# A selective scan on VectorE: two halves of the channels in one product, one scan and one multiplication by C

## The reference, cut to what matters

```python
# u_c, z: [token, 256]; dt_r, Bm, Cm come from u_c @ W_x.T (8, 16 and 16 columns)
dt = jax.nn.softplus(jnp.einsum('blr,dr->bld', dt_r, W_dt) + b_dt)
A = -jnp.exp(A_log)                                   # [256 channels, 16 states]
def step(h, inp):                                     # over the 256 tokens of a sequence
    dt_t, u_t, B_t, C_t = inp
    dA = jnp.exp(dt_t[..., None] * A)
    h = dA * h + (dt_t * u_t)[..., None] * B_t[:, None, :]
    y_t = jnp.einsum('bds,bs->bd', h, C_t)
    return (h, y_t)
y = (ys + u_c * D) * jax.nn.silu(z)
out = jnp.einsum('bld,ed->ble', y, W_out)
```

## Time and profile before

| | |
|---|---|
| Time, median of 3 runs | 628.76 us (628.01 to 629.89) |
| The profiled execution: its own time / its span | 627.47 us / 626.1 us |
| Scan phase, first drive to last scan | 279.1 to 526.7 us |
| Busy from 279 to 527 us (248 us): PE / DVE / ACT / POOL | 212.4 / 244.4 / 150.5 / 195.9 us |
| Busy from 527 to 626 us (99 us): PE / DVE / ACT / POOL | 83.0 / 36.9 / 30.9 / 26.7 us |
| Granted TensorE clock, as a share of full speed | 0.912 over the span, 0.96 in the scan phase |

### The profile page before, as it was taken

How to read it: one execution, slowest core, us unless ns; L and a number is a source line. 1 busy time by engine, 2 the same in 40 slices (tenths; PEclk the granted TensorE clock), 3 DMA queues, 4 the chain that set the end, 5 groups by cost and what they waited for, 6 DMA issues and landing times.

```text
span 626.1 us, 7242 instructions
## 1 busy us (share of the span) xinstructions
PE 516.1 (82%) x2146; PEld 285.0 (46%) x2146; DVE 445.5 (71%) x858; ACT 302.9 (48%) x562; POOL 314.0 (50%) x276
## 2 busy tenths in 40 slices
PE   1985777888877989889898998888787887679897
PEld 0732444556646855543233433323332432448655
DVE  5289978687232435549999999999999998424343
ACT  2654345345142532486774865755557541325421
POOL 0048433342441027026789778877899766310072
PEclk9996788788658999989999999989989898699999
DMA  8999900000003332021222121222221220023312
GB/s 299 413 332 331 311 30 1 1 1 19 21 28 106 112 90 54 6 70 58 79 71 69 67 66 67 72 63 71 83 67 68 84 69 4 17 69 93 115 51 85
DMA packets 31879, 58.09 MB, mean 93 GB/s; under 512 B 4384, under 2 KB 20256, under 8 KB 30944
## 3 DMA queue, kind: packets, MB, share of 16 engines
q1 hardware_dynamic: 29504, 52.06, 25.5%
q0 software_dynamic: 2048, 4.20, 2.4%
q10 hardware_dynamic: 288, 1.37, 0.7%
HBM read 50.27 MB, written 26.15 MB: 122 GB/s over the span
## 4 chain that ended last, share of the span: by engine, by line
PE 38%; DVE 29%; issue 11%; ACT 9%; POOL 8%; DMA 3%; SPq 2%; DVEq 0%; POOLq 0%; ACTq 0%
DVE arena L1275 10%; PE psum L663 7%; POOL arena L1780 5%; PE psum L714 4%; PE psum L859 4%; DVE psum L1269 4%; DVE arena L1092 3%; PE psum L673 3%; PE psum L735 3%; PE psum L773 3%; ACT L1347 2%; PE psum L435 2%; POOL by_expert L1706 2%; DVE stats L927 1%; PE psum L424 1%
## 5 line engine op out<-in xcount | busy, mean ns | idle before, releaser
L1780 POOL TENSOR_TENSOR arena<-arena 128x512 f32<-128x512 f32 x128 | 160.3, 1276 | 50.5 <-DVE arena L1275 50.0
L859 PE MATMUL psum<-arena,w 128*128 128x512 f32 x256 | 137.3, 645 | 19.9 <-POOL arena L1780 13.1
L1275 DVE TENSOR_TENSOR_SCAN arena<-arena,psum 128x512 f32<-128x512 f32 x128 | 148.2, 1196 | 0.5 <-DVE psum L1269 0.3
L1621 ACT ACTIVATE arena<-arena 128x510 f32<-128x510 f32 x128 | 87.8, 715 | 55.9 <-DVE arena L1275 54.2
L1269 DVE TENSOR_TENSOR psum<-psum,arena 128x512 f32<-128x512 f32 x128 | 81.3, 678 | 2.0 <-PE psum L850 1.9
L859 PEld LDWEIGHTS psum<-arena,w 128*128 128x128 f32 x256 | 44.6, 196 | 75.7 <-POOL arena L1780 50.2
L1724 POOL DMA_INDIRECT arena<-by_expert,routes x32 | 30.7, 959 | 91.0 <-DMA by_expert<-arena 81.9
L663 PE MATMUL psum<-xnt,w 128*128 128x512 f32 x128 | 62.7, 646 | 0.9 <-DVE arena L1145 0.9
L1674 POOL TENSOR_TENSOR arena<-arena 128x512 f32<-128x512 f32 x16 | 20.3, 1267 | 85.6 <-DVE arena L988 85.6
L850 PE MATMUL psum<-arena,c 96*128 96x512 bf16 x128 | 43.8, 399 | 16.8 <-DVE arena L1275 13.9
L1145 DVE TENSOR_TENSOR arena<-psum,arena 128x512 f32<-128x512 f32 x32 | 22.0, 690 | 30.0 <-PE psum L663 28.9
(11 more groups left out here) (184 smaller groups left out, 868.2 us busy)
## 6 DMA issues: line engine op xcount, KB each, us to landing
by_expert<-w_in SPq DMA_DIRECT2D x4, 4096.0 KB, 45.2
arena<-c_store SPq DMA_DIRECT2D x64, 256.0 KB, 3.1
w<-w_in SPq DMA_DIRECT2D x1, 4427.5 KB, 13.3
arena<-by_expert SPq DMA_DIRECT2D x62, 64.0 KB, 1.8
by_expert<-arena SPq DMA_DIRECT2D x62, 64.0 KB, 1.6
by_expert<-w_in SPq DMA_DIRECT2D x1, 1984.0 KB, 69.5
x<-x_in SPq DMA_DIRECT2D x4, 256.0 KB, 7.7
c<-c_in SPq DMA_DIRECT2D x1, 1024.0 KB, 15.4
```

The lines of the kernel that those rows point to most:

```text
L859: nc.tensor.matmul(bank(6 + c), ident, state[c][s % 3], start=(n == 0), stop=(n == DS - 1)).then_inc(*summed.inc((s, c)))
L1275: nc.vector.tensor_tensor_scan(state[c][s % 3], decay_b[c][s % 2], bank(2 * c + s % 2), 0.0, ALU.mult, ALU.add).then_inc(*state_ready.inc( ...
L1621: nc.scalar.activation(live, seq, ACT.Exp, scale=a_neg[:, DS * c + n:DS * c + n + 1]).then_inc(*decay_ready.inc((s, c)))
L1780: nc.gpsimd.tensor_tensor(state[c][s % 3], state[c][s % 3], c_row[s % len(c_row)], ALU.mult).then_inc(*y_done.inc((s, c)))
```

## The change

The drive, the scan and the multiplication by C now take both halves in one instruction of 1024 columns. The two banks of a step lie side by side (`drive_bank`: banks 2 and 3 for even steps, 0 and 1 for odd ones), and `decay_b` and `state` hold both halves in one piece. The second half's decays begin with a zero too, so the scan runs on from the first half into the second without carrying anything over. The signals `b_ready`, `decay_ready`, `driven`, `state_ready` and `y_done` exist once a step instead of once a half. PE's picks, ACT's exponentials and PE's sums remain one for each half. The first difference of the rows of groups 1 to 3 moves from DVE to GpSimd's `split`, which now stands one step earlier.

```diff
+        def drive_bank(s):
+            return NCH * ((s + 1) % 2)
...
-        decay_b = [[piece(BANK) for _ in range(2)] for _ in range(NCH)]
-        state = [[piece(BANK) for _ in range(3)] for _ in range(NCH)]
+        decay_b = [piece(NCH * BANK) for _ in range(2)]
+        state = [piece(NCH * BANK) for _ in range(3)]
...
-        ready_dve = {0: ("measure", 3), 2: ("centre", 3), 7: ("rest", 1), 20: ("rest", 2), 34: ("rest", 3)}
-        ready_pool = {8: ("split", 1), 13: ("drive", 1), 21: ("split", 2), 27: ("drive", 2), 35: ("split", 3), 43: ("drive", 3)}
+        ready_dve = {0: ("measure", 3), 2: ("centre", 3)}
+        ready_pool = {7: ("split", 1), 13: ("drive", 1), 20: ("split", 2), 27: ("drive", 2), 34: ("split", 3), 43: ("drive", 3)}
...
# PE, prepare(s): picks
+                    if s >= 2:
+                        pe.wait_ge(*state_ready[s - 2])
                     for c in range(NCH):
-                        pe.wait_ge(*(state_ready[s - 2, c] if s >= 2 else bank_free[s, c]))
-                        nc.tensor.matmul(bank(2 * c + s % 2), pick_row[:, P * n:P * n + P], rows16[:, group(g)],
-                                         start=True, stop=True).then_inc(*b_ready.inc((s, c)))
+                        if s < 2:
+                            pe.wait_ge(*bank_free[s, c])
+                        r = nc.tensor.matmul(bank(drive_bank(s) + c), pick_row[:, P * n:P * n + P], rows16[:, group(g)], start=True, stop=True)
+                    r.then_inc(*b_ready.inc(s))
# PE, add_up(s): sums
-                        pe.wait_ge(*y_done[s, c])
-                        nc.tensor.matmul(bank(6 + c), ident, state[c][s % 3], start=(n == 0), stop=(n == DS - 1)).then_inc(*summed.inc((s, c)))
+                        if c == 0:
+                            pe.wait_ge(*y_done[s])
+                        nc.tensor.matmul(bank(6 + c), ident, state[s % 3][:, BANK * c:BANK * c + BANK], start=(n == 0), stop=(n == DS - 1)).then_inc(*summed.inc((s, c)))
# DVE, recur(s)
-                    for c in range(NCH):
-                        to = bank(2 * c + s % 2)
...
-                        dve.wait_ge(*b_ready[s, c])
-                        nc.vector.tensor_tensor(to, to, dtu[:, c, group(g)], ALU.mult).then_inc(*driven.inc((s, c)))
-                    for c in range(NCH):
-                        dve.wait_ge(*driven[s, c])
-                        dve.wait_ge(*decay_ready[s, c])
-                        if s >= 3:
-                            dve.wait_ge(*summed[s - 3, c])
-                        nc.vector.tensor_tensor_scan(state[c][s % 3], decay_b[c][s % 2], bank(2 * c + s % 2), 0.0,
-                                                     ALU.mult, ALU.add).then_inc(*state_ready.inc((s, c)))
+                    at = drive_bank(s)
+                    drives = psum[:, at:at + NCH, :]
...
+                    dve.wait_ge(*b_ready[s])
+                    nc.vector.tensor_tensor(drives, drives, dtu[:, :, group(g)], ALU.mult).then_inc(*driven.inc(s))
+                    dve.wait_ge(*decay_ready[s])
+                    if s >= 3:
+                        dve.wait_ge(*summed[s - 3, NCH - 1])
+                    dve.wait_ge(*driven[s])
+                    nc.vector.tensor_tensor_scan(state[s % 3], decay_b[s % 2], drives.rearrange("p c t -> p (c t)"), 0.0,
+                                                 ALU.mult, ALU.add).then_inc(*state_ready.inc(s))
# GpSimd, split(g)
+                if g >= 1:
+                    pool.wait_ge(*c_copied[g])
+                    nc.gpsimd.tensor_tensor(re, c_rows[g % 2], rows16[0:2 * DS, group(g)], ALU.subtract).then_inc(*rest_ready.inc(g))
                 pool.wait_ge(*rest_ready[g])
# GpSimd, the steps
-                for c in range(NCH):
-                    if s < n_steps:
-                        pool.wait_ge(*state_ready[s, c])
-                        pool.wait_ge(*c_loaded[s % len(c_row)][s])
-                        nc.gpsimd.tensor_tensor(state[c][s % 3], state[c][s % 3], c_row[s % len(c_row)], ALU.mult).then_inc(*y_done.inc((s, c)))
+                if s < n_steps:
+                    states = state[s % 3].rearrange("p (c t) -> p c t", c=NCH)
+                    pool.wait_ge(*c_loaded[s % len(c_row)][s])
+                    pool.wait_ge(*state_ready[s])
+                    nc.gpsimd.tensor_tensor(states, states, c_row[s % len(c_row)].unsqueeze(1).to_broadcast([P, NCH, BANK]),
+                                            ALU.mult).then_inc(*y_done.inc(s))
```

More of the change, by code:

```diff
@@ L395, in build @@
         step_events = range(n_steps)
-        both = [(s, c) for s in step_events for c in range(NCH)]
-        b_ready, driven, state_ready, y_done, summed = (signal(n, both) for n in ("b_ready", "driven", "state_ready", "y_done", "summed"))
-        decay_ready = signal("decay_ready", both)
+        b_ready, decay_ready, driven, state_ready, y_done = (
+            signal(n, step_events) for n in ("b_ready", "decay_ready", "driven", "state_ready", "y_done"))
+        summed = signal("summed", [(s, c) for s in step_events for c in range(NCH)])
         c_copied, c_stored = signal("c_copied", GROUPS), signal("c_stored", GROUPS, 16)
@@ L412, in build @@
         last = n_steps - 1
-        exit_b = [summed[last, NCH - 1], skipped[NGRP - 1, NCH - 1], y_done[last, NCH - 1]]
+        exit_b = [summed[last, NCH - 1], skipped[NGRP - 1, NCH - 1], y_done[last]]
         def tensor_program():
@@ L896, in pending @@
                     rank(3, NGRP - 1, end_ring)
-                rings = [Ring([bank(i), bank(i + 1)], [state_ready[n_steps - 2, i // 2], state_ready[n_steps - 1, i // 2]]) for i in (0, 2)]
+                rings = [Ring([bank(drive_bank(s) + c) for c in range(NCH)], [state_ready[s]] * NCH) for s in (n_steps - 2, n_steps - 1)]
                 return pending, *rings, Ring([bank(6), bank(7)], [skipped[NGRP - 1, c] for c in range(NCH)])
@@ L1244, in enter_scan @@
                 nc.vector.tensor_scalar(a_neg, a_neg, -1.0, None, ALU.mult).then_inc(*a_neg_set.inc(0))
-                for c in range(NCH):
-                    for i in range(2):
-                        starts = decay_b[c][i].rearrange("p (s t) -> p s t", t=SEQ)[:, :, 0:1]
-                        r = nc.vector.memset(starts, 0.0)
+                for decays in decay_b:
+                    r = nc.vector.memset(decays.rearrange("p (s t) -> p s t", t=SEQ)[:, :, 0:1], 0.0)
                 r.then_inc(*starts_set.inc(0))
                 scale(2, 2)
-                rest_of(0)
+                first_rest()
                 add_last()
@@ L1299, in selective_scan @@
                             centre_on(2, g)
-                        elif what == "rest":
-                            rest_of(g)
                     for what, g in due_in_steps(s):
@@ L1614, in prepare @@
                     for c in range(NCH):
-                        live = decay_b[c][s % 2].rearrange("p (s t) -> p s t", t=SEQ)[:, :, 1:SEQ]
+                        live = decay_b[s % 2][:, BANK * c:BANK * c + BANK].rearrange("p (s t) -> p s t", t=SEQ)[:, :, 1:SEQ]
                         seq = dt_b[:, c, group(g)].rearrange("p (s t) -> p s t", t=SEQ)[:, :, 1:SEQ]
-                        if s >= 2:
-                            act.wait_ge(*state_ready[s - 2, c])
+                        if s >= 2 and c == 0:
+                            act.wait_ge(*state_ready[s - 2])
                         if n == 0 and g >= 1:
                             act.wait_ge(*dtb_ready[g])
-                        nc.scalar.activation(live, seq, ACT.Exp, scale=a_neg[:, DS * c + n:DS * c + n + 1]).then_inc(*decay_ready.inc((s, c)))
+                        r = nc.scalar.activation(live, seq, ACT.Exp, scale=a_neg[:, DS * c + n:DS * c + n + 1])
+                    r.then_inc(*decay_ready.inc(s))
                 for s in range(-1, n_steps + 1):
@@ L1821, in spread_rows @@
                     if s >= len(c_row):
-                        sp.wait_ge(*y_done[s - len(c_row), NCH - 1])
+                        sp.wait_ge(*y_done[s - len(c_row)])
                     at = DS * g + n
```

17 lines of the change are left out of this document (6 added, 11 removed).

## The result

The changed kernel takes 647.27 us (median of 4 runs, 644.9 to 648.58), the kernel before in the same comparison 628.38 us (4 runs, 627.49 to 629.89): a ratio of 1.0294, 95% interval 1.0253 to 1.0334. It is slower by 18.9 us, where +3.5 was forecast (632.3 us) and the range ended at 638 us. The profiled execution took 646.17 us, its span is 644.8.

A forecast was written before the change was run, and what follows sets the result against it. DVE's queue was taken as the bound. Terms 0 - 7.6 + 0.7 + 1.8 + 4.1 + 1.7 + 1.0 + 1.8 = +3.5 us on 627.47 gave 631.0, plus 1.3 for the median: 632.3 us; range 627.8 to 638.

The forecast's parts named there:

- Part 4: GpSimd's backlogs delay PE's sums and picks, so DVE waits: +0.7 (step 11), +1.8 (17), +4.1 (36, 38), +1.7 us (52).
- Rival C: PE's passes run slower behind each new wait, with 0.05 a step on DVE: +3 to +6, 635 to 638 us; chance 0.22.
- Part 1: Merged drive and scan on DVE: step stays 3.42 us, gain 0; bounds +3 and -7 us.
- Rival A: Merging saves fixed costs on DVE, 0.29 us a step, partly lost to waits: about 623.5 us; chance 0.1.
- Part 5: ACT's decays, released by the whole scan, come late at three places: +1.0 us, bounds 0 and 2.
- Part 3: GpSimd's merged multiplication by C takes 2346 ns, gaining 0.15 us a step, but starts only after the whole scan.
- rival B: GpSimd's merged multiplication by C is cheap, 1933 ns, so each lag falls: 626.5 us; chance 0.08.
- Part 2: The difference leaves DVE: -7.6 us, of which 5.86 is a single one, counted only if nothing else stops DVE there.
- Part 6: Tail from the last scan's end to the last skip grows from 2.7 to 4.5 us: +1.8.
- Rival D: DVE's waits behind GpSimd's backlogs are smaller than worked out, the moved difference's gain stays whole: 627 to 629.5 us; chance 0.17.

The follow-up runs named there:

- experiment 3: Changed kernel plus eleven products by zero on PE ahead of the sums of six steps: ratio 1.0265 to the kernel before; of eleven steps: 652.48 us, 1.0346.
- experiment 1: Kernel before with only the first difference of groups 1 to 3 moved from DVE to GpSimd's split, all in halves: 625.34 us, ratio 0.996.

## Why the prediction was wrong, step by step

**The bound and the direction** held: slower, DVE's queue is the path, and GpSimd's lag reaches it through PE's sums and picks. The places were mostly right too: steps 11, 17, 36, 38 and 52 hold 14.1 of the 16.1 us. The size failed, in two steps.

**Part 4 failed most, in the price of PE's work behind a late y.** It priced everything that PE does behind a late y at full speed: "four passes of the sums 1.71", 0.86 a projection, two picks 0.44. Measured at step 11: 2.73, 2.07 and 1.03. New waits were to be 8.3 us; they are 14.2. The forecast for step 11 was 0.7, it is 2.96; step 17: 3.3, it is 4.54; steps 36 and 38: 4.1, they are 3.5; step 52: 2.1, it is 3.1.

How long PE takes from the first sum behind the late y to the next drive can be read at each place. Part 4 has 3.21 us at step 11 (1.71 + 0.86 + 0.44 + 0.2), 4.06 at step 17, 2.35 at step 36, 3.21 at steps 38 and 52. The changed kernel's trace has 5.73, 5.87, 4.15, 3.61 and 5.01, together 8.3 us more. The waits at these five places are 3.9 us above the forecast; why the rest of this longer time on PE didn't come through is not worked out. The other 2.0 of the 5.9 us by which the waits exceed the forecast lie at steps 12, 31, 47 and 48, where part 4 had no wait. The largest of these is the 1.15 us at step 47, behind drive(3) of step 43, which was said to "stay under the limit"; there PE took 4.67 us, where its prices give 2.35, and began with the slowest sums of all:

```profile
464.74 3.78 PE L867 MATMUL psum<-arena,w 128*128 128x512 f32 x4 [4.21 <-POOL arena L1783]
```

Rival C named the mechanism and gave it 3 us at most besides its 0.05 a step. At steps 11 and 17 alone 3.8 us go with the lower clock (experiment 3), and it was low at three more: 0.57 from 419 to 423 us (step 36), 0.50 from 464 to 470 (step 47), 0.69 from 486 to 491 (step 52). It was 1.00 from 425 to 435, where step 38 has the time nearest to its price. At full clock, too, the work behind a wait took longer than priced, 3.61 us against 3.21 at step 11. Why the clock falls at some of these places stays open.

**Part 1 failed by 0.12 us a step, in the price of the dependence.** The term "starts 0.04 us after its end" came from the earlier trace rows, where the second instruction has one wait. The scan has three, with the product's last, and starts after 0.12; with the product's first, after 0.04. That is 0.08. The other 0.04 is the scan itself, 2.29 us long instead of 2.24. Together 7.6 us, well over the +3 that was this part's upper bound. Rival A had no hold: the step never fell below 3.42. (Its own sum was off by a little: 18.6 less 4 and 5 leaves 9.6, so 622.7 and not 623.5.)
The Trainium skill (VectorE: DVE Perf Modes, The DRAIN you can't avoid) says of a row of VectorE copies that a semaphore after each costs nothing extra. No run here leaves a semaphore out, but a wait for the instruction directly ahead has a price in this trace: the start lies 0.12 or 0.04 us behind that instruction's end, by the order of the waits, and 0.08 before it where the instruction ahead isn't the one waited for.

**Part 5, and what was not counted.** The scans' waits for ACT are 2.0 us in 5 places against an estimate of 1.0 and a bound of 2. The casts held by GpSimd, +2.3 us, had no term. One of them:

```profile
531.34 2.10 DVE L984 CAST routes<-routes 128x4 int32<-128x4 f32 x1
```

```profile
531.07 2.35 POOL L1783 TENSOR_TENSOR arena<-arena 128x1024 f32<-128x1024 f32 x1 [1.19 <-DVE arena L1276]
```

The cast ends with the multiplication (533.44 and 533.42). This last cast takes 2.10 or 2.11 us in every kernel of which the multiplication by C is merged, and 0.96 to 1.07 in those that have it in halves, where GpSimd's instructions are 1.25 us long.

**What held.** Part 3: 2354 ns, forecast 2346; rival B had no hold. Part 2: -7.6 us on DVE, and that the 5.86 had covered a wait (experiment 1). Part 6: +1.9, forecast +1.8. The chain behind the last scan:

```profile
540.69 2.34 POOL arena L1783
```

```profile
539.54 5.51 PE L867 MATMUL psum<-arena,w 128*128 128x512 f32 x8 [4.09 <-POOL arena L1783]
```

GpSimd ends at 543.03 and PE's last four passes at 545.05; the skip of the second half follows, and ends at 545.84. Rival D had no hold for the changed kernel.

By measured ratios: C merged alone 1.0163; with product and scan merged as well 1.0296; all three parts 1.0294; the difference alone 0.996.

## What to carry to other kernels

Merging two instructions saves their fixed cost only if the program paid it: where independent instructions stand between a producer and its consumer, the engine overlaps them already, and the merged pair loses that cover. In a pipeline over several engines the merged instruction also hands its result over later, so count the lag at the places where the engine behind it is already late, and price what follows there with a range: the same work of PE took 3.6 us at full clock and 5.7 us with the clock at 0.74. Of several waits ahead of one instruction, put the one that ends last first; this showed in the gap between the instructions, not in the time of the kernel.

## What the hardware showed that was not expected

- The order of three waits ahead of one DVE instruction is worth 0.08 us: it starts 0.12 us after its producer's end when the producer's wait is the last of them, 0.04 when it is the first.
- Behind waits of 3 to 4 us the next passes of PE took up to 1.9 times as long at many places (four sums 3.78 us instead of 1.98), with a granted clock of 0.50 to 0.84 in such stretches; behind waits of 2.87 and 2.96 us in another trace they took 1.98 at a clock of 1.00. With eleven small products in the idle time there were both outcomes as well.
- Three programs that are the same up to step 34 (the difference alone, with the split behind step 34, 40 and 36) waited 2.0, 3.8 and 6.2 us for picks before 350 us, with granted clocks of 0.93, 0.86 and 0.73 in 300 to 325. A single trace's waits are no closer than that.
- Some DVE instructions on SBUF (the difference, the centring, the cast) didn't finish while GpSimd was at work beside them: 5.86, 2.73 and 2.10 us, where the same take 0.7, 0.3 and 0.2 otherwise. The centring and the cast ended within 0.03 us of GpSimd's end.
